# Maxima and exponentials ahead of the rounding of folded weights in steps 0 to 2 of an attention and expert layer

## The chip, the cores and the metric

One core of a Trainium2 chip runs the whole layer in one launch. The metric is the device time of an execution in microseconds (us), lower is better. The kernel before took 949.34 us, the median of 3 runs (948.89 to 950.56).

## The reference

The layer is one pre-norm block on x of 8 x 512 x 128, all in fp32. First attention with 16 heads of 64, whose keys and values come through a low-rank projection; then a mixture of 8 experts of which each token uses 2.

```python
h = layernorm(x)
kv = (h @ w_kv_down) @ w_kv_up            # 128 -> 128 -> 2048
k, v = kv[..., :1024], kv[..., 1024:]
q = h @ w_q                               # 128 -> 1024
att = softmax(causal(q k^T * 64 ** -0.5)) # 16 heads of 64, 512 x 512
x = x + (att v) @ w_out                   # 1024 -> 128
h = layernorm(x)
# logits = h @ Wr; the two largest, softmax over them
x = x + sum over the 2 chosen experts e of weight_e * (silu(h @ Wg[e]) * (h @ Wu[e])) @ Wd[e] * 12 ** -0.5
```

## The kernel before, in words

The kernel writes each engine's program out by hand, one block per engine: SyncE (SP) for most loads and stores, GpSimd (POOL), ScalarE (ACT), VectorE (DVE) and TensorE (PE). Each engine works strictly through its own list, and the lists meet through counting semaphores: `seen(eng, S[...], n)` or `wait_ge` makes an engine stop until a counter has reached n.

**Folded weights.** The product of w_kv_down and w_kv_up is made once, on chip: `fold` (L918) lets PE multiply one 512-column part (k0, v0, v1, k1) into PSUM. So that matmuls can run on a faster fp32 format without loss, every operand is held as a rounded high part and a low part that is the remainder. `w_hi` (L434) is ScalarE's rounding of a 512-column half of a weight into `Wb`, and counts `whi_done`; `w_lo` (L623) is VectorE's subtraction of that from the original, also into `Wb`, and counts `wlo_done`. The second halves of k and q are `w_lo(Wk, 1, 5, ...)`, from PSUM bank `post_ps`, and `w_lo(Wq, 1, 6, ...)`, from `w_q_sb`, which lies in SBUF in the space of `W_ffn`. The q and k of a step are split in the same way by `qk_hi` (ScalarE, L454) and `qk_lo` (VectorE, L657).

**Steps.** Attention runs in 64 steps: 8 batch rows with 8 pairs of heads each. A step n works on one pair for 512 tokens, in four pieces i of 128 queries, whose keys grow with i from 128 to 512, in the order 1, 0, 2, 3. For each piece: scores on PE (L970), maxima on VectorE with the causal mask added (`maxes`, L639), exponentials on ScalarE (`exps`, L465), reciprocal of their sums on VectorE (`inv`, L646), normalisation on GpSimd (`norm`, L333), transposes on PE (L984), their copy to SBUF on VectorE (`t_copy`, L651; piece 3 on ScalarE, `t3_copy`, L471). In the step after, PE multiplies by V (`values`, L997), ScalarE copies the result (`y_copy`) and PE projects it (`project_out`, L1004). One step ahead PE projects q and k (`project`, L925 to L927), three ahead V (`v_chunk`, the same lines), copied by ScalarE (L476).

**The opening.** Step 0 is written out apart from the others on each engine: ScalarE's from `qk_hi(0)` (L527) on, VectorE's from `qk_lo(0)` (L796) on, PE's from `fold("k0", ...)` on (L1081). PE's list there is: scores of step 0, fold v0, q and k for step 1, fold v1, four V chunks, transposes of pieces 1, 2 and 0, fold k1, transposes of piece 3, then the common `step`. The transposes of piece 2 wait for VectorE's copy of piece 1's. The matmuls of step 1's scores wait for nothing of the second halves of k and q; `project(4)`, which PE issues in step 3, waits for `wlo_done` 6.

**Other queues.** SyncE waits for `wlo_done` 6 as well (L249) and then loads the experts' first weights, 16 loads, into `W_ffn` (L251, L252); then it waits for all nine fills before it loads the second ones (L255). GpSimd issues a fill of the routed rows in DRAM (`fill`, L367) behind the normalisations of each of the steps 0 to 7, and a last one, and waits for all nine (L391) before step 9. From step 54 on the expert weights are split into high and low parts in the same way (`split_hi` L510, `split_lo` L707). After attention a table of the routed rows is made and 71 tiles of 128 rows go through the experts.

Of the kernel before, what the change touches and what calls it, by code (L numbers as in the profile page):

```python
# [16 lines left out]
B, T, C = 8, 512, 128  # L17
# [27 lines left out]
def seen(eng, sem, count):  # L45

    if not isinstance(count, int) or count > 0:
        eng.wait_ge(sem, count)
# [11 lines left out]
def layer(nc, x, w_down, w_up, w_q, w_out, Wr, Wg, Wu, Wd, out):  # L60
    ctx = ExitStack()
    with ctx:
# [88 lines left out]
        w_q_sb = W_ffn[:, 2, :]  # L151
        w_down_sb = W_ffn[:, 4, 0:R]

        Wq, Wk, Wv = ([Wb[:, a, :] for a in blocks] for blocks in ((2, 3), (6, 7), (0, 4)))
# [6 lines left out]
        post_ps = ctx.enter_context(nc.psum_tensor("post_ps", [P, T], F32))  # L161
# [22 lines left out]
        def p_at(i, h):  # L184

            o = 128 * i * (i + 1) + h * 128 * (i + 1)
            return prob[:, o:o + 128 * (i + 1)]
# [242 lines left out]
        def _(act):  # L430
# [3 lines left out]
            def w_hi(W, half, ps=None):  # L434

                if ps is None:
                    act.wait_ge(w_in[f"q{half}"], 16)
                    ps = w_q_sb[:, half * T:(half + 1) * T]
                nc.scalar.activation(W[0][:, half * T:(half + 1) * T], ps, ACT.Copy).then_inc(S["whi_done"], 1)
# [10 lines left out]
            def qk_hi(n):  # L450

                for a in range(2):
                    seen(act, S["qk_ready"], 2 * n + a + 1)
                    nc.scalar.activation(qk_sb[:, 0, a, :], mid_ps[:, a * T:(a + 1) * T], ACT.Copy).then_inc(S["qkhi_done"], 1)  # L454
# [6 lines left out]
            def exps(n, i):  # L461

                for h in range(2):
                    seen(act, S["max_done"], 8 * n + 2 * POS[i] + h + 1)
                    nc.scalar.activation(p_at(i, h), p_at(i, h), ACT.Exp, bias=neg_max[:, i, h:h + 1], scale=-1.0,  # L465
                                         accum_out=row_sum[:, i, h:h + 1]).then_inc(S["exp_done"], 1)
# [6 lines left out]
            def v_copy(n, half, t, bank=0):  # L473

                seen(act, S["v_ready"], n + 1)
                nc.scalar.activation(v_sb[:, half, t, :], mid_ps[:, bank * T:(bank + 1) * T], ACT.Copy).then_inc(S["v_copied"], 1)  # L476
# [51 lines left out]
            step0 = [(t % 2, t) for t in range(NT)]  # L528
            exps(0, 1)
            exps(0, 0)  # L530
            act.wait_ge(S["kv_ready"], 2)
            w_hi(Wv, 0, post_ps[:, :])
            exps(0, 2)
            qk_hi(1)
            act.wait_ge(S["kv_ready"], 3)
            w_hi(Wv, 1, post_ps[:, :])
            for bank, t in step0:
                v_copy(t, 0, t, bank)
            exps(0, 3)
            act.wait_ge(S["kv_ready"], 4)  # L540
            w_hi(Wk, 1, post_ps[:, :])
            t3_copy(0)
# [54 lines left out]
        def _(dve):  # L597
            dve.wait_ge(consts, 5)

            def pre_stats(b):  # L600
                dve.wait_ge(x_in[b], 16)
                for t in range(NT):
                    nc.vector.bn_stats(stats_a[:, t, :], X[:, NT * b + t, :])\
                        .then_inc(S["stats_a"], 1)
                seen(dve, S["stats_a"], NT * b + NT)
                for t in range(NT):
                    nc.vector.bn_aggr(mv_a[:, t, :], stats_a[:, t, :]).then_inc(S["aggr_a"], 1)
# [15 lines left out]
            def w_lo(W, half, count, ps):  # L623

                dve.wait_ge(S["whi_done"], count)
                o = slice(half * T, (half + 1) * T)
                nc.vector.tensor_tensor(W[1][:, o], ps, W[0][:, o].bitcast(F32), ALU.subtract).then_inc(S["wlo_done"], 1)
# [15 lines left out]
            def inv(n, i):  # L643

                seen(dve, S["exp_done"], 8 * n + 2 * POS[i] + 2)
                nc.vector.reciprocal(row_inv[:, i, :], row_sum[:, i, :]).then_inc(S["inv_done"], 1)  # L646

            def t_copy(n, i):

                seen(dve, S[f"t{i}_ready"], n + 1)  # L650
                nc.vector.tensor_copy(pt_sb(i), pt_ps(i)).then_inc(S[f"t{i}_copied"], 1)  # L651

            def qk_lo(n):

                for a in range(2):
                    seen(dve, S["qkhi_done"], 2 * n + a + 1)
                    nc.vector.tensor_tensor(qk_sb[:, 1, a, :], mid_ps[:, a * T:(a + 1) * T], qk_sb[:, 0, a, :].bitcast(F32),  # L657
                                            ALU.subtract).then_inc(S["qklo_done"], 1)

            def step(n, k, cur=True, nxt=True, pre=None, post=None):  # L660
                if cur:
                    maxes(n, 1)
                    maxes(n, 0)
                    maxes(n, 2)
                    inv(n, 1)
                    maxes(n, 3)
                    inv(n, 0)
                    inv(n, 2)

                if n - 1 in SPLIT_AT and cur:  # L670
                    split_lo(SPLIT_AT[n - 1])
                if pre is not None and k == 1:
                    pre_stats(pre)
                if post is not None and k == 2:
                    post_x2(post)
                if pre is not None and k == 3:
                    pre_norm(pre)
                if post is not None and k == 4:
                    post_xn2(post)
                if post is not None and k == 5:  # L680
                    post_choose(post)
                if post is not None and k == 7:
                    post_weights(post)
                if cur:
                    inv(n, 3)
                    t_copy(n, 1)
                if nxt:
                    qk_lo(n + 1)
                if cur:
                    t_copy(n, 2)  # L690
                    t_copy(n, 0)

                if post is not None and k == 2:
                    post_stats(post)
                if post is not None and k == 3:
                    post_aggr(post)
                if pre is not None and k == 3:
                    pre_lo(pre)
                if post is not None and k == 5:
                    post_chosen(post)  # L700
                if post is not None and k == 6:
                    post_rows(post)

            def split_lo(e):

                dve.wait_ge(S["split_hi"], SPLIT_ORDER.index(e) + 1)
                nc.vector.tensor_tensor(up_lo[:, e, :], W_ffn[:, e, :], up_hi[:, e, :].bitcast(F32), ALU.subtract)\  # L707
                    .then_inc(S["split_lo"], 1)
# [88 lines left out]
            for i in (1, 0, 2):  # L797
                maxes(0, i)
            inv(0, 1)
            w_lo(Wv, 0, 3, post_ps[:, :])  # L800
            maxes(0, 3)
            inv(0, 0)
            inv(0, 2)
            qk_lo(1)
            w_lo(Wv, 1, 4, post_ps[:, :])
            inv(0, 3)
            for i in (1, 2, 0):
                t_copy(0, i)
            w_lo(Wk, 1, 5, post_ps[:, :])
            w_lo(Wq, 1, 6, w_q_sb[:, T:2 * T])  # L810
            for k in range(1, NP + 1):
                step(k, k, pre=1)
            for m in range(1, B - 1):
# [398 lines left out]
```

## Time and profile before

| | |
|---|---|
| median of 3 runs | 949.34 us (948.89 to 950.56) |
| profiled execution, its own time | 950.33 us |
| its span, first to last instruction | 948.5 us |
| PE busy | 882.4 us, 93% |
| VectorE busy | 665.7 us, 70% |
| ScalarE busy | 620.1 us, 65% |
| GpSimd busy | 541.9 us, 57% |
| chain of work that ended last | PE 79%, VectorE 13%, GpSimd 4% |

The profile is of one execution. Its span is a little shorter than the execution's time, which has some 1.8 us around it. PE is the weight-streaming matrix engine; a busy PE is a PE with matmuls in flight. A timeline row gives start and length in us, the engine, the line of the kernel, the operation, what it writes and reads, how many instructions were merged, and in brackets the idle time of the engine before it and what ended it. "PEclk" or the granted clock is the share of full speed that TensorE's clock had.

### The profile page before, as it was taken

What the parts mean: (1) busy time and instruction counts of PE and PEld (TensorE: products, weight loads), DVE (VectorE), ACT (ScalarE), POOL (GpSimd) and SP (SyncE); (2) the same over time, 40 slices, a digit from 0 to 9 for tenths busy, and PEclk for the clock granted to TensorE, in tenths of its full rate; (3) what the DMA queues carried; (4) which work ended last, traced back from release to release, by engine and by line L of the source; (5) the groups of instructions that cost most, each with busy time, mean ns of one, the idle gap of its engine ahead of it and who ended that gap; (6) DMA issues with size and microseconds to landing.
All of it is one profiled execution on the core that took longest, in us unless ns stands there. A gap on an engine that the chain in (4) does not pass through costs nothing.

```text
span 948.5 us, 20447 instructions
## 1 busy us (share of the span) xinstructions
PE 882.4 (93%) x6126; PEld 647.6 (68%) x6127; DVE 665.7 (70%) x2442; ACT 620.1 (65%) x1614; POOL 541.9 (57%) x536
## 2 busy tenths in 40 slices
PE   6799999999999999999999999999842999999996
PEld 3566666676666667676666767676522888888885
DVE  3576788878788887878888787877853444554552
ACT  3577687777768777776877777777721455445553
POOL 3455544585566558556655855665553466665555
PEclk9999999999999999999999999999975999999998
DMA  6585430000000000000000000000011233333332
GB/s 180 181 326 212 184 101 1 1 24 13 1 11 26 1 2 23 12 2 12 24 1 1 25 12 1 11 26 1 2 34 37 35 48 49 45 45 45 45 44 28
DMA packets 43996, 44.36 MB, mean 47 GB/s; under 512 B 4352, under 2 KB 35968, under 8 KB 43920
## 3 DMA queue, kind: packets, MB, share of 16 engines
q0 software_dynamic: 16528, 26.03, 11.4%
q1 hardware_dynamic: 27392, 17.39, 6.7%
q8 instruction: 40, 0.66, 0.3%
q14 instruction: 36, 0.29, 0.1%
HBM read 15.28 MB, written 28.12 MB: 46 GB/s over the span
## 4 chain that ended last, share of the span: by engine, by line
PE 79%; DVE 13%; POOL 4%; issue 2%; ACT 1%; DMA 0%; POOLq 0%; SPq 0%; DVEq 0%
PE low_ps L997 11%; PE low_ps L984 7%; PE low_ps L1149 7%; PE mid_ps L925 7%; DVE prob L639 6%; PE top_ps L984 6%; PE mid_ps L927 6%; PE mid_ps L926 6%; PE out_ps L1004 5%; PE mid_ps L970 4%; PE out_ps L1141 4%; PE low_ps L970 4%; PE top_ps L970 3%; DVE routed L733 2%; DVE PT L613 2%
## 5 line engine op out<-in xcount | busy, mean ns | idle before, releaser
L333 POOL TENSOR_TENSOR prob<-prob,row_inv 128x512 f32<-128x512 f32 (+3 forms) x256 | 321.6, 1273 | 263.2 <-DVE row_inv L646 263.2
L465 ACT ACTIVATE prob<-prob,neg_max 128x256 f32<-128x256 f32 (+3 forms) x512 | 280.6, 550 | 10.3 <-DVE neg_max L639 3.8
L997 PE MATMUL low_ps<-PT,v_sb 128*64 128x512 f32 (+3 forms) x1024 | 152.0, 439 | 2.1 <-ACT PT L471 1.2
L997 PEld LDWEIGHTS low_ps<-PT,v_sb 128*64 128x64 f32 x1024 | 68.1, 136 | 94.1 <-issue 60.4
L414 POOL DMA_INDIRECT out<-prob,meta_row x71 | 110.6, 1558 | 36.2 <-issue 35.7
L651 DVE COPY PT<-low_ps 128x512 f32<-128x512 f32 (+1 forms) x128 | 104.6, 817 | 31.9 <-PE low_ps L984 30.8
L984 PEld LDWEIGHTS low_ps<-ident,prob 128*128 128x128 f32 x640 | 75.2, 141 | 57.7 <-POOL prob L333 27.5
L882 DVE TENSOR_TENSOR prob<-mid_ps,prob 128x512 f32<-128x512 f32 x71 | 49.1, 692 | 91.6 <-ACT prob L570 84.6
L476 ACT ACTIVATE v_sb<-mid_ps 128x512 f32<-128x512 f32 x64 | 38.3, 598 | 103.0 <-PE mid_ps L927 102.8
L639 DVE CUSTOM_DVE_ANT_0 prob<-mid_ps,mask 128x128 f32<-128x128 f32 (+1 forms) x256 | 93.7, 421 | 6.7 <-PE mid_ps L970 0.8
L984 PE MATMUL low_ps<-ident,prob 128*128 128x128 f32 x640 | 92.2, 275 | 6.2 <-DVE PT L651 5.2
L465 ACT ACTIVATION_READ_ACCUMULATOR prob<-prob,neg_max 128x1 f32 x512 | 95.6, 187 | 0.0
L471 ACT ACTIVATE PT<-top_ps 128x1024 f32<-128x1024 f32 x64 | 65.7, 1027 | 44.6 <-PE top_ps L984 44.6
L639 DVE CUSTOM_DVE_ANT_0 prob<-low_ps,mask 128x256 f32<-128x256 f32 x128 | 49.2, 422 | 54.6 <-PE low_ps L970 54.6
L657 DVE TENSOR_TENSOR qk_sb<-mid_ps,qk_sb 128x512 fp32r<-128x512 f32 x128 | 81.9, 679 | 2.9 <-ACT qk_sb L454 2.9
L564 ACT ACTIVATE xT_sb<-post_ps 128x128 fp32r<-128x128 f32 x71 | 19.8, 278 | 95.1 <-PE post_ps L1120 95.1
L639 DVE CUSTOM_DVE_ANT_0 prob<-top_ps,mask 128x512 f32<-128x512 f32 x128 | 81.9, 678 | 0.0
L349 POOL DMA_INDIRECT routed_rows<-routed,row_i x64 | 64.0, 1001 | 16.5 <-issue 16.5
L454 ACT ACTIVATE qk_sb<-mid_ps 128x512 fp32r<-128x512 f32 x128 | 67.9, 580 | 3.2 <-PE mid_ps L927 3.2
L1004 PE MATMUL out_ps<-y_sb,Wo_sb 128*128 128x512 f32 x128 | 66.7, 603 | 2.1 <-ACT y_sb L459 2.1
L984 PE MATMUL top_ps<-ident,prob 128*128 128x128 f32 x512 | 67.1, 274 | 0.7 <-POOL prob L333 0.7
L970 PE MATMUL mid_ps<-qk_sb 64*128 64x128 f32 (+1 forms) x768 | 66.2, 305 | 0.0
(172 smaller groups left out, 1773.7 us busy)
## 6 DMA issues: line engine op xcount, KB each, us to landing
routed_rows<-W_dn POOLq DMA_DIRECT2D x8, 2080.0 KB, 8.9
routed<-routed_rows SPq DMA_DIRECT2D x71, 65.0 KB, 1.9
X<-in_L_attn_x SPq DMA_DIRECT2D x8, 256.0 KB, 5.5
W_ffn<-in_L_ffn_Wg SPq DMA_DIRECT2D x8, 256.0 KB, 5.1
W_ffn<-in_L_ffn_Wu SPq DMA_DIRECT2D x8, 256.0 KB, 5.4
W_dn<-in_L_ffn_Wd SPq DMA_DIRECT2D x8, 256.0 KB, 4.6
out<-X SPq DMA_DIRECT2D x8, 256.0 KB, 2.3
out<-prob,meta_row POOLq DMA_INDIRECT x71, 3.3
```

The costliest lines, as they stand in the source:

```text
L333: nc.gpsimd.tensor_tensor(p_pair(i), p_pair(i), row_inv[:, i, :].unsqueeze(2).to_broadcast([P, 2, P * (i + 1)]), ALU.mult).then_inc(S["nor ...
L414: nc.gpsimd.indirect_dma_start(out=out, out_offset=bass.IndirectOffsetOnAxis(ap=meta_row[:, q:q + 1], axis=0), in_=eo_sb[q], in_offset=Non ...
L454: nc.scalar.activation(qk_sb[:, 0, a, :], mid_ps[:, a * T:(a + 1) * T], ACT.Copy).then_inc(S["qkhi_done"], 1)
L465: nc.scalar.activation(p_at(i, h), p_at(i, h), ACT.Exp, bias=neg_max[:, i, h:h + 1], scale=-1.0, accum_out=row_sum[:, i, h:h + 1]).then_in ...
L639: nc.vector.tensor_tensor_reduce(out=p_at(i, h), in0=scores_at(i, h), in1=mask[:, T - w:T], scale=-SCALE, scalar=BIG, op0=ALU.add, op1=ALU ...
L651: nc.vector.tensor_copy(pt_sb(i), pt_ps(i)).then_inc(S[f"t{i}_copied"], 1)
L657: nc.vector.tensor_tensor(qk_sb[:, 1, a, :], mid_ps[:, a * T:(a + 1) * T], qk_sb[:, 0, a, :].bitcast(F32), ALU.subtract).then_inc(S["qklo_ ...
L925: nc.tensor.matmul(dst, ws[0], vs[0], start=start, stop=False, **kw)
L970: last = nc.tensor.matmul(scores_at(i, h), qk_sb[d, a, 0, i * P:(i + 1) * P], qk_sb[d, b, 1, 0:P * (i + 1)], start=(k == 0), stop=(k == 2))
L984: last = nc.tensor.transpose(pt_ps(i)[:, h, j, :], p_at(i, h)[:, j * P:(j + 1) * P], ident[:, :])
L997: last = nc.tensor.matmul(y_ps[h * HD:(h + 1) * HD, j * P:T], v_sb[:, half, j, o + h * HD:o + (h + 1) * HD], PT[:, h, j, j:NT, :].rearrang ...
L1004: nc.tensor.matmul(out_ps[:, :], Wo_sb[:, pair, :], y_sb[:, :], start=(pair == 0), stop=(pair == NP - 1), skip_group_check=True).then_inc( ...
```

## The change

On ScalarE the exponentials of piece 2 of step 0 go ahead of the rounding of the first V half, and those of piece 3 ahead of the rounding of step 1's q and k, that is ahead of the second V half's rounding and of four V copies. On VectorE the maxima of piece 3 and the reciprocals of pieces 0, 2 and 3 go ahead of the subtraction for the first V half or directly behind it, ahead of `qk_lo(1)`. The subtraction for the second k half goes from the end of step 0 to behind the copies of step 1, and that for the second q half to step 2, behind the maxima and ahead of the reciprocal of piece 3. PE's, GpSimd's and SyncE's programs are the same.

```diff
--- before.py
+++ after.py
@@ -528,15 +528,15 @@
             step0 = [(t % 2, t) for t in range(NT)]
             exps(0, 1)
             exps(0, 0)
+            exps(0, 2)
             act.wait_ge(S["kv_ready"], 2)
             w_hi(Wv, 0, post_ps[:, :])
-            exps(0, 2)
+            exps(0, 3)
             qk_hi(1)
             act.wait_ge(S["kv_ready"], 3)
             w_hi(Wv, 1, post_ps[:, :])
             for bank, t in step0:
                 v_copy(t, 0, t, bank)
-            exps(0, 3)
             act.wait_ge(S["kv_ready"], 4)
             w_hi(Wk, 1, post_ps[:, :])
             t3_copy(0)
@@ -671,6 +671,8 @@
                     split_lo(SPLIT_AT[n - 1])
                 if pre is not None and k == 1:
                     pre_stats(pre)
+                if n == 2:
+                    w_lo(Wq, 1, 6, w_q_sb[:, T:2 * T])
                 if post is not None and k == 2:
                     post_x2(post)
                 if pre is not None and k == 3:
@@ -690,6 +692,8 @@
                     t_copy(n, 2)
                     t_copy(n, 0)
 
+                if n == 1:
+                    w_lo(Wk, 1, 5, post_ps[:, :])
                 if post is not None and k == 2:
                     post_stats(post)
                 if post is not None and k == 3:
@@ -797,17 +801,15 @@
             for i in (1, 0, 2):
                 maxes(0, i)
             inv(0, 1)
-            w_lo(Wv, 0, 3, post_ps[:, :])
             maxes(0, 3)
             inv(0, 0)
             inv(0, 2)
+            w_lo(Wv, 0, 3, post_ps[:, :])
+            inv(0, 3)
             qk_lo(1)
             w_lo(Wv, 1, 4, post_ps[:, :])
-            inv(0, 3)
             for i in (1, 2, 0):
                 t_copy(0, i)
-            w_lo(Wk, 1, 5, post_ps[:, :])
-            w_lo(Wq, 1, 6, w_q_sb[:, T:2 * T])
             for k in range(1, NP + 1):
                 step(k, k, pre=1)
             for m in range(1, B - 1):
```

## Rows read from the trace of the kernel before

**Rows 1.** The page: each engine's busy time, share of the span, instructions.

```profile
PE 882.4 (93%) x6126; PEld 647.6 (68%) x6127; DVE 665.7 (70%) x2442; ACT 620.1 (65%) x1614; POOL 541.9 (57%) x536
```

**Rows 2.** PE's timeline: start, length, line, operation, count, idle time before and its end.

```profile
25.58 0.50 PE L925 MATMUL mid_ps<-Wb,XT 128*128 128x512 f32 x1 [1.41 <-DVE qk_sb L657]
...
28.73 0.60 PE L984 MATMUL low_ps<-ident,prob 128*128 128x128 f32 x4
...
31.86 1.17 PE L984 MATMUL low_ps<-ident,prob 128*128 128x128 f32 x6 [2.53 <-DVE PT L651]
...
36.27 0.62 PE L970 MATMUL low_ps<-qk_sb 64*128 64x256 f32 x6
...
44.03 1.13 PE L1004 MATMUL out_ps<-y_sb,Wo_sb 128*128 128x512 f32 x2 [0.25 <-ACT y_sb L459]
...
47.53 0.62 PE L970 MATMUL low_ps<-qk_sb 64*128 64x256 f32 x6
...
56.51 1.04 PE L984 MATMUL top_ps<-ident,prob 128*128 128x128 f32 x8
```

**Rows 3.** ScalarE's timeline in steps 0 and 1.

```profile
22.16 0.61 ACT L465 ACTIVATE prob<-prob,neg_max 128x384 f32<-128x384 f32 x1
...
23.36 1.07 ACT L454 ACTIVATE qk_sb<-mid_ps 128x512 fp32r<-128x512 f32 x2
...
29.43 0.71 ACT L465 ACTIVATE prob<-prob,neg_max 128x512 f32<-128x512 f32 x1
...
37.30 0.62 ACT L439 ACTIVATE Wb<-W_ffn 128x512 fp32r<-128x512 f32 x1
...
39.02 0.51 ACT L465 ACTIVATE prob<-prob,neg_max 128x256 f32<-128x256 f32 x1 [1.10 <-DVE neg_max L639]
```

**Rows 4.** VectorE's timeline in steps 0 to 2.

```profile
24.26 1.27 DVE L657 TENSOR_TENSOR qk_sb<-mid_ps,qk_sb 128x512 fp32r<-128x512 f32 x2
...
30.96 0.17 DVE L646 RECIPROCAL row_inv<-row_sum 128x2 f32<-128x2 f32 x1 [4.84 <-ACT prob L465]
...
31.05 0.67 DVE L651 COPY PT<-low_ps 128x512 f32<-128x512 f32 x1
...
37.96 0.69 DVE L627 TENSOR_TENSOR Wb<-W_ffn,Wb 128x512 fp32r<-128x512 f32 x1 [1.43 <-ACT Wb L439]
...
48.30 0.43 DVE L639 CUSTOM_DVE_ANT_0 prob<-low_ps,mask 128x256 f32<-128x256 f32 x1 [1.11 <-PE low_ps L970]
...
53.28 0.17 DVE L646 RECIPROCAL row_inv<-row_sum 128x2 f32<-128x2 f32 x1 [1.23 <-ACT prob L465]
```

**Rows 5.** PE in half-microsecond slices: slice, length, busy, granted clock, DMA share, GB/s.

```profile
32.00:32.50 0.50, 0.50 (x5) 0.74 0.00 0
...
33.00:33.50 0.50, 0.50 (x4) 0.50 0.00 0
...
35.50:36.00 0.50, 0.50 (x6) 0.85 1.01 408
```

**Rows 6.** GpSimd's timeline, four places.

```profile
24.36 2.04 POOL L333 TENSOR_TENSOR prob<-prob,row_inv 128x256 f32<-128x256 f32 x2 [3.25 <-DVE row_inv L646]
...
52.07 3.89 POOL L333 TENSOR_TENSOR prob<-prob,row_inv 128x256 f32<-128x256 f32 x3 [0.24 <-DVE row_inv L646]
...
121.54 1.03 POOL L333 TENSOR_TENSOR prob<-prob,row_inv 128x512 f32<-128x512 f32 x1 [4.31 <-DVE row_inv L646]
...
600.49 3.00 POOL L333 TENSOR_TENSOR prob<-prob,row_inv 128x256 f32<-128x256 f32 x2 [0.24 <-DVE row_inv L646]
```

**Rows 7.** VectorE's timeline at the split of an expert weight.

```profile
600.39 1.20 DVE L707 TENSOR_TENSOR XT<-W_ffn,Wb 128x1024 fp32r<-128x1024 f32 x1
```

**Rows 8.** SyncE's timeline, its waits for wlo_done and for the fills behind it.

```profile
38.67 0.34 SPq L251 DMA_DIRECT2D W_ffn<-in_L_ffn_Wg  x1
...
118.60 5.91 SPq L255 DMA_DIRECT2D W_dn<-in_L_ffn_Wd  x8
```

**Rows 9.** Windows of 2 us, all engines: busy each, granted clock, DMA share, GB/s.

```profile
104.00:106.00 2.00, 1.98 (x11) 1.10 (x10) 1.31 (x3) 1.44 (x3) 2.00 (x2) 1.00 0.00 0
```

## The prediction

> **What bounds the kernel now.** I read the page first: PE is busy 882.4 of 948.5 us [rows 1], so a microsecond can be won only where PE stands still, where it runs slowly, or by letting its unbroken work begin sooner. Then I read PE's timeline. From about 44 us on, PE passes from step to step with hardly a gap; from one step's first scores matmul (36.27, then 47.53) to the next is a fixed round, and whatever is won before step 2 should shift all that follows. The change touches only the stretch from 19 to 54 us, so that is where I look.
>
> In it PE stands still at three places that the change could reach: 1.41 us ahead of the first V matmul at 25.58, 2.53 us ahead of the transposes of piece 2 at 31.86, and, in step 1, in the long round from the scores at 36.27 to the output projection at 44.03, 7.76 us [rows 2]. The 2.53 us gap is a chain through four engines. ScalarE first takes the exponentials of piece 3 at 29.43, since it has them behind four V copies; VectorE stands 4.84 us waiting for them, for its reciprocal at 30.96, and the copy of piece 1's transposes, ready since 29.33 (28.73 + 0.60), is queued behind it and starts at 31.05; PE's next transposes want that copy [rows 2, 3, 4].
>
> The clock is the second thing to see. PE's granted clock is full until the gap, goes to the lower level at about 32.26 (0.74 over the slice 32.0 to 32.5 is 52% at full and 48% at half) and is back at about 35.65 (0.85 over 35.5 to 36.0); between them the slices read 0.50, 1.2 GHz in place of 2.4 [rows 5]. PE was busy all through those 3.4 us, so at full clock the same work takes half, 1.7 us less. The 1.41 us gap before 25.58 brought no such fall.
>
> **The change part by part.**
>
> *Exponentials of pieces 2 and 3 earlier on ScalarE, V rounding behind them.* Piece 2's go into time in which ScalarE waited for PE's fold of the first V half; that rounding still ends where the row at 22.16 starts. Piece 3's then take about 1.4 us of ScalarE (two of 0.71 from 29.43; VectorE is released at 30.96) and the q and k roundings of step 1 start at 22.16 + 1.41 = 23.57 in place of 23.36, 0.2 us later [rows 3, 4]. VectorE starts the subtraction on them at 23.57 + 0.60 = 24.17; before, it started at 24.26, because the maxima of piece 3 lay behind the V subtraction [rows 3, 4]. Now those maxima come first, in time that VectorE spent waiting for ScalarE's V rounding, and the V subtraction still follows that rounding at once. So the V matmuls start within 0.1 us of 25.58. I cost this at nothing. Its bounds: 0.1 us won, and 0.3 us lost if the reciprocal of piece 3, which now stands ahead of the q and k subtraction, is released late.
>
> *The reciprocal of piece 3* is made at about 23.8, and what waited behind it at 30.96 is free. The copy of piece 1's transposes starts when PE has made them, 29.35; PE starts 0.81 us after a copy starts (31.05 to 31.86), so at 30.16 [rows 2, 4]. Won: 31.86 - 30.16 = **1.7 us**. GpSimd's normalisations for pieces 0, 2 and 3 must be there: the first two took 2.04 us from 24.36 and can now only be earlier, and the third takes 3.89 - 2.04 = 1.85 (all three of a step are 3.89), so even with the old start all is done by 28.3 [rows 6]. GpSimd's first fill DMA then goes out some 5 to 7 us sooner, which can only bring the end of the fills forward.
>
> *The clock.* The idle time before these transposes is now 0.83 us, less than the 1.41 us that caused no fall. So I take the clock to stay full, and the slow stretch goes: **1.7 us**. Bounds: 0, if it falls all the same, and 1.7, since all of it is gone then.
>
> *The k and q subtractions out of the end of step 0.* At 37.96 VectorE made the last of them (q), released only by ScalarE's rounding at 37.30, and the maxima of step 1 stood behind it, though their scores were ready at 36.9; ScalarE's first exponential of step 1 was at 39.02, 2.75 us behind the scores' start at 36.27 [rows 2, 3, 4]. Now the maxima start with the scores, and ScalarE is late next: the q rounding is still ahead of its exponentials, starts 1.03 us behind the scores' start (37.30) and takes 0.53 of its time (half of the pair of 1.07 at 23.36), so the first exponential comes at +1.56. From the first exponential to the projection it is 44.03 - 39.02 = 5.01 us of ScalarE's own work, unchanged: 6.57 in place of 7.76. Won: **1.2 us**. Bounds: 0.4 (if something else holds the maxima for two thirds of that) and 1.4 (PE's own round).
>
> *The k subtraction in step 1* costs VectorE 0.6 us behind its last copy; there VectorE was idle for 1.11 us until the maxima at 48.30 [rows 4]. Hidden, 0.5 us to spare; with that cover gone it would cost 0.6. *The q subtraction in step 2* stands ahead of a reciprocal for which VectorE waited 1.23 us, at 53.28 [rows 4]. Hidden, 0.6 to spare. Nothing uses the second halves of q and k before the projection for step 4, which PE issues in step 3.
>
> It does meet GpSimd, though. A subtraction with both inputs in SBUF at 600.39 (1.20 us) ran beside two normalisations of the same widths together that took 3.00 us, where such two take 2.04 at 24.36: GpSimd lost 0.96 us, and VectorE nothing [rows 6, 7]. The q subtraction is such an instruction of half the length, and starts with the normalisations of step 2 (52.07, 3.89 us, ending 55.96), so these end about 0.5 us later, at 56.45; PE wants the last of them at 56.51 [rows 2, 6]. Cost 0, bound 0.5. The Trainium skill has this as a rule (SBUF — State Buffer, section "SBUF: two separate sides"): VectorE with two SBUF inputs and a GpSimd instruction that reads SBUF exclude one another for the whole instruction, whichever comes first. The trace agrees for the case with VectorE first; if GpSimd came first with two normalisations, VectorE would by that rule wait 2.04 us, 1.4 more than it has to spare, and the sum would be 3.2 us.
>
> *The expert weights.* SyncE waits for the sixth subtraction before it loads them: from 38.67 to about 48, some 9 us later [rows 8]. They are first used in step 54. Cost nothing.
>
> **Sum:** 1.7 + 1.7 + 1.2 = 4.6 us. The profiled execution took 950.33 us (span 948.5 and 1.8 around it), so a like one would take 945.7. The median of the runs shown is 949.34, 1.0 lower; I take the difference from that: **944.7 us**.
>
> **The rivals.**
>
> *The clock is not saved* (12%). Either it falls after 0.83 us too, or it does not fall in every execution of the kernel before: the runs shown spread over 1.7 us, as much as one slow stretch costs, and the profiled one, which holds a fall, is the second slowest of the four. If so, most executions win only the waits. Then 2.9 us are won, 946.4. The Trainium skill says that the gate's moments are not tied to the kernel, so that one kernel shows different numbers of slow matmuls (TensorE: Matmul & The Clock Gate, "What's actually happening"); no two executions are shown here by which to test it.
>
> *The gain is given back* (8%). PE stands still again between attention and the experts, with the clock low, and the execution could regain its clock there a slow stretch later, 1.7 us; together with only the 2.9 us above it is 948.1, no measurable change. Or a wait that I do not see takes the place of the reciprocal's: the row of 4.84 us hides what else was late behind it. Against it: the other inputs of those transposes are ready 4 us before.
>
> *Slower, by the fills* (4%). GpSimd stops before step 9 until all nine fills of the routed rows have landed. They had by 118.60, when SyncE's next loads went out on the same condition, and were needed at 121.54, 2.9 us of margin [rows 6, 8]. The expert weights, 16 loads of 256 KB, now fall on the fills some 9 us later. If that made the last fill late by more than 2.9 us, each further microsecond would hold the normalisations and PE. To be slower than before it must be more than 2.9 + 4.6 us late; 10 us late gives 951.8. Against it: between two fills the queues are empty (share 0.00 from 104 to 106 us), so the backlog is gone long before [rows 9].
>
> *The change doesn't do what it says* (4%): the order on one engine moves and another, later wait decides; within 1 us of before, 948.5.
>
> **How the numbers follow.** Forecast 72%. A measurement of this kernel can tell about 0.2%, 1.9 us, from no change. The forecast and the first rival lie beyond it with room (4.6 and 2.9 us), with some loss for the spread of the runs: faster 0.86; the second and the last give within 0.2%: 0.10; slower 0.04. The range reaches down to 943.2, the sum with its bounds of gain (0.3 us) and the spread of the median (some 1 us), and up to 947.3, the first rival with the same spread.
>
> **What would show it.** Right: the idle time ahead of the transposes of piece 2 is 0.8 us and no slice around 30 to 36 us has a clock under 1.00; the first V matmul stays at 25.5; the scores of step 1 start at 32.9, the first exponential of step 1 1.6 us later, the first projection at 39.4 and the scores of step 2 at 42.9; in step 2 GpSimd's three normalisations take 4.4 in place of 3.89 us; the expert weights go out at 48. Wrong: a fall of the clock in front of the V matmuls; VectorE late for the maxima of step 2; a gap on PE in step 2 ahead of the transposes of piece 3; GpSimd waiting for a DMA before step 9; or a low clock that lasts longer in the stage before the experts.

## The result and the profile after

| | before | after |
|---|---|---|
| median, measured together, 20 runs each | 951.0 us (948.89 to 953.77) | 947.99 us (945.48 to 950.70) |
| ratio after to before, 95% interval | | 0.9971 (0.9961 to 0.9981) |
| profiled execution, its own time | 950.33 us | 946.45 us |
| its span | 948.5 us | 944.7 us |
| PE busy | 882.4 us | 880.3 us |

The change is faster by 0.29%, 3.0 us (1.8 to 3.7 by the interval), where 4.6 was forecast. In the range's own terms the time missed it, 947.99 against at most 947.3; of that, 1.7 us is the kernel before, whose median over 20 runs is 951.0 and not the 949.34 of the first three.

The part of the page of the kernel after that answers to [rows 1], each engine's busy time:

```profile
PE 880.3 (93%) x6126; PEld 646.6 (68%) x6127; DVE 666.2 (71%) x2442; ACT 620.4 (66%) x1614; POOL 542.4 (57%) x536
```

PE's timeline of the kernel after in steps 0 to 2, the lines that answer to [rows 2] (start, length, line, operation, count, idle time before and its end):

```profile
15.74 0.62 PE L972 MATMUL low_ps<-qk_sb 64*128 64x256 f32 x6 [1.41 <-DVE qk_sb L657]
...
21.20 1.13 PE L923 MATMUL post_ps<-W_ffn,wdT 128*128 128x512 f32 x2 [0.77 <-DVE Wb L627]
...
23.69 0.50 PE L927 MATMUL mid_ps<-Wb,XT 128*128 128x512 f32 x1 [1.36 <-DVE qk_sb L657]
...
26.84 0.60 PE L986 MATMUL low_ps<-ident,prob 128*128 128x128 f32 x4
...
28.32 0.84 PE L986 MATMUL low_ps<-ident,prob 128*128 128x128 f32 x6 [0.87 <-DVE PT L651]
...
31.04 0.63 PE L972 MATMUL low_ps<-qk_sb 64*128 64x256 f32 x6
...
37.58 1.12 PE L1006 MATMUL out_ps<-y_sb,Wo_sb 128*128 128x512 f32 x2
...
41.08 0.63 PE L972 MATMUL low_ps<-qk_sb 64*128 64x256 f32 x6
...
50.07 1.04 PE L986 MATMUL top_ps<-ident,prob 128*128 128x128 f32 x8
```

What to see: the wait ahead of the transposes of piece 2 is 0.87 us in place of 2.53. From the scores of step 1 to the projection there are 37.58 - 31.04 = 6.54 us (before 7.76), and PE does not wait for the projection any more. From the scores of step 1 to those of step 2 it is 10.04 us, before 11.26. But the first V matmul starts at 23.69, not at 25.5, and there is a new wait of 0.77 us ahead of the v1 fold. This execution differs from that of [rows 2] before the change comes into play: its first six score matmuls of step 0 took 0.62 us at 15.74, and in the profile before they took 1.01:

```profile
15.73 1.01 PE L970 MATMUL low_ps<-qk_sb 64*128 64x256 f32 x6 [1.41 <-DVE qk_sb L657]
```

ScalarE's timeline of the kernel after, answering to [rows 3]:

```profile
19.85 0.58 ACT L439 ACTIVATE Wb<-post_ps 128x512 fp32r<-128x512 f32 x1
...
20.32 0.71 ACT L465 ACTIVATE prob<-prob,neg_max 128x512 f32<-128x512 f32 x1
...
21.73 1.06 ACT L454 ACTIVATE qk_sb<-mid_ps 128x512 fp32r<-128x512 f32 x2
...
32.07 0.62 ACT L439 ACTIVATE Wb<-W_ffn 128x512 fp32r<-128x512 f32 x1
...
32.59 0.50 ACT L465 ACTIVATE prob<-prob,neg_max 128x256 f32<-128x256 f32 x1
```

Piece 3's exponentials (20.32, two with 0.71 between their starts) stand between the V rounding and the roundings of q and k at 21.73. In step 1 the first exponential starts at 31.04 + 1.55, behind the q rounding, as forecast (1.56).

VectorE's, answering to [rows 4]:

```profile
21.86 0.17 DVE L646 RECIPROCAL row_inv<-row_sum 128x2 f32<-128x2 f32 x1 [0.72 <-ACT prob L465]
...
22.34 1.29 DVE L657 TENSOR_TENSOR qk_sb<-mid_ps,qk_sb 128x512 fp32r<-128x512 f32 x2 [0.31 <-ACT qk_sb L454]
...
27.48 0.69 DVE L651 COPY PT<-low_ps 128x512 f32<-128x512 f32 x1 [3.25 <-PE low_ps L986]
...
40.66 0.68 DVE L627 TENSOR_TENSOR Wb<-post_ps,Wb 128x512 fp32r<-128x512 f32 x1
...
41.86 0.42 DVE L639 CUSTOM_DVE_ANT_0 prob<-low_ps,mask 128x256 f32<-128x256 f32 x1 [0.52 <-PE low_ps L972]
...
45.52 0.67 DVE L627 TENSOR_TENSOR Wb<-W_ffn,Wb 128x512 fp32r<-128x512 f32 x1
...
46.83 0.17 DVE L646 RECIPROCAL row_inv<-row_sum 128x2 f32<-128x2 f32 x1 [0.64 <-ACT prob L465]
```

The copy at 27.48 waits for PE alone. Both moved subtractions (40.66 and 45.52) are hidden, with 0.52 and 0.64 us of idle time left behind them.

GpSimd's in step 2 and SyncE's, answering to [rows 6, 8]:

```profile
45.63 4.33 POOL L333 TENSOR_TENSOR prob<-prob,row_inv 128x256 f32<-128x256 f32 x3 [0.24 <-DVE row_inv L646]
...
46.23 0.34 SPq L251 DMA_DIRECT2D W_ffn<-in_L_ffn_Wg  x1
...
112.32 5.49 SPq L255 DMA_DIRECT2D W_dn<-in_L_ffn_Wd  x8
```

The three normalisations of step 2 take 4.33 us in place of 3.89, by the subtraction at 45.52, and nothing waits for them: the transposes of piece 3 at 50.07 have no idle time before them.

At the scores of step 2 this trace is 47.53 - 41.08 = 6.45 us ahead of the one before, at the end of the span only 3.8. The start of each step's scores, which I read from both timelines, shows where 2.1 us went: steps 17, 25, 41 and 56 took 10.90, 10.77, 10.83 and 10.75 us in place of 10.23, 10.21, 10.24 and 10.48. So neither the 6.45 nor the 3.8 is the price of the change. The experiments had to take chance and change apart.

### The profile page after: what moved, and what is told of

It reads as the page before. It is cut to its first block, busy times and chain, and to the rows that moved or that the text cites. A ratio compares the mean times of both kernels' runs of the same rounds, so it can differ in the third digit from the quotient of the medians.

```text
span 944.7 us, 20447 instructions
## 1 busy us (share of the span) xinstructions
PE 880.3 (93%) x6126; PEld 646.6 (68%) x6127; DVE 666.2 (71%) x2442; ACT 620.4 (66%) x1614; POOL 542.4 (57%) x536
## 4 chain that ended last, share of the span: by engine, by line
PE 77%; DVE 12%; issue 4%; ACT 3%; POOL 2%; POOLq 0%; DMA 0%; SPq 0%; DVEq 0%
PE low_ps L999 10%; PE low_ps L986 7%; PE low_ps L1151 7%; PE mid_ps L927 6%; DVE prob L639 6%; PE top_ps L986 6%; PE out_ps L1006 6%; PE mid_ps L929 5%; PE mid_ps L928 5%; PE out_ps L1143 4%; PE mid_ps L972 4%; PE low_ps L972 4%; PE top_ps L972 3%; DVE PT L613 2%; ACT prob L465 2%
## 5 line engine op out<-in xcount | busy, mean ns | idle before, releaser
L651 DVE COPY PT<-low_ps 128x512 f32<-128x512 f32 (+1 forms) x128 | 104.6, 817 | 34.9 <-PE low_ps L986 34.1
```

## The experiments

Each kernel was measured beside the kernel before on the same chip. Three chips were used, and the medians of the kernel before were 947.98, 947.87 and 947.62 us there. Where a range in us is given for a difference, it is worked out from the 95% interval of the ratio. In all traces I read the same six places in the opening; "slow" is a PE whose six matmuls of step 0's first scores take 1.01 us, "fast" one where they take 0.62.

| trace | PE in step 0 | first V matmul | wait ahead of piece 2's transposes | clock behind it | scores of step 1 | of step 2 |
|---|---|---|---|---|---|---|
| before | slow | 25.58 | 2.53 | falls | 36.27 | 47.53 |
| before, second | fast | 22.92 | 2.53 | stays | 31.94 | 43.20 |
| before, third | fast | 22.91 | 2.53 | stays | 31.95 | 43.20 |
| after | fast | 23.69 | 0.87 | stays | 31.04 | 41.08 |
| after, second | fast | 23.70 | 0.88 | stays | 31.05 | 41.10 |
| after, third | fast | 23.66 | 0.88 | stays | 31.01 | 41.05 |
| order alone | slow | 25.26 | 0.88 | stays | 32.62 | 43.88 |
| subtractions alone | slow | 24.79 | 2.53 | stays | 33.80 | 43.85 |
| busy gap | slow | 25.24 | 0.69 | stays | 34.27 | 45.53 |
| copy first | slow | 24.70 | 0.88 | stays | 33.32 | 44.58 |
| q and k first | fast | 22.37 | 0.88 | stays | 29.73 | 39.77 |
| before with fillers | fast | 21.13 | 2.53 | falls | 31.82 | 43.07 |
| after with fillers | fast | 21.88 | 0.87 | stays | 29.24 | 39.28 |
| q and k first, with fillers | fast | 20.58 | 0.88 | stays | 27.93 | 37.98 |

"Stays" and "falls" speak of the stretch behind that wait alone; later falls are told further down. One column less another takes the chance of the opening out: from the first V matmul to the scores of step 1 it is 9.0 us in every kernel with the old order and no fall, 10.7 where the clock fell, and 7.35 with the new order. So the wait is worth 1.65 us and a fall 1.7.

### The order of step 0 alone

The changed kernel, with the two subtractions back where they were:

```diff
             for i in (1, 2, 0):
                 t_copy(0, i)
+            w_lo(Wk, 1, 5, post_ps[:, :])
+            w_lo(Wq, 1, 6, w_q_sb[:, T:2 * T])
...
-                if n == 2:
-                    w_lo(Wq, 1, 6, w_q_sb[:, T:2 * T])
...
-                if n == 1:
-                    w_lo(Wk, 1, 5, post_ps[:, :])
```

> Only the new order inside step 0 (exponentials, maxima and reciprocals ahead of the V rounding); the k and q subtractions stay at the end of step 0. Theory A (my sum: the wait is 1.7 us, and a fall of the clock in the gap costs another 1.7): the gap ahead of the transposes of piece 2 shrinks from 2.5 to 0.8 us, no slice from 26 to 38 us has a clock under 1.00, and the execution is 3.4 us shorter than before. Rival B (the fall of the clock in that gap is not in every execution of the kernel before): the same trace, but the median is nearer to 1.7 to 2.5 us shorter. Rival C (what was won at the opening is lost again in steps in which GpSimd issues scatters): less than 1.5 us shorter, with single steps some 0.6 us longer than 10.2.

Measured: 945.61 us against 947.98, ratio 0.9979 (0.9967 to 0.9992), so 2.0 us shorter (0.8 to 3.1). PE's timeline of this kernel:

```profile
15.75 1.01 PE L970 MATMUL low_ps<-qk_sb 64*128 64x256 f32 x6 [1.41 <-DVE qk_sb L657]
...
25.26 0.50 PE L925 MATMUL mid_ps<-Wb,XT 128*128 128x512 f32 x1 [1.36 <-DVE qk_sb L657]
...
29.89 0.85 PE L984 MATMUL low_ps<-ident,prob 128*128 128x128 f32 x6 [0.88 <-DVE PT L651]
...
32.62 0.64 PE L970 MATMUL low_ps<-qk_sb 64*128 64x256 f32 x6
...
35.73 1.73 PE L997 MATMUL low_ps<-PT,v_sb 128*64 128x512 f32 x8 [0.92 <-DVE neg_max L639]
```

The wait is 0.88 us, and nothing falls behind it; the wait of 0.92 us ahead of the values in step 1 is left, since the subtractions still stand ahead of the maxima. The amount is rival B's: 1.65 us for the wait and little more. Theory A's 3.4 lies outside the interval, if by little.

### The subtractions alone

```diff
-            w_lo(Wk, 1, 5, post_ps[:, :])
-            w_lo(Wq, 1, 6, w_q_sb[:, T:2 * T])
...
+                if n == 2:
+                    w_lo(Wq, 1, 6, w_q_sb[:, T:2 * T])
...
+                if n == 1:
+                    w_lo(Wk, 1, 5, post_ps[:, :])
```

> Only the k and q subtractions moved to steps 1 and 2; the order inside step 0 is the old one. Theory A: 1.2 us shorter than before, the 2.5 us gap is still there, with a slow clock behind it in some or all executions; from the scores of step 1 to the scores of step 2 it is 10.0 in place of 11.3 us. Rival: 0, if the q rounding on ScalarE, which still stands ahead of step 1's exponentials, sets them all the same.

Measured: 947.06 us, ratio 0.999 (0.9977 to 1.0003): not to be told from 0, and in keeping with 1.2 us. Step 1 shows it: 10.05 us to the scores of step 2 in place of 11.26, so 1.21 us. What matters more is PE's timeline ahead of that, and PE in windows of 2 us (window, length, busy, granted clock, DMA share, GB/s):

```profile
31.07 0.85 PE L986 MATMUL low_ps<-ident,prob 128*128 128x128 f32 x6 [2.53 <-DVE PT L651]
```

```profile
29.00:31.00 2.00, 0.00 (x0) 1.00 0.00 0
...
31.00:33.00 2.00, 1.93 (x12) 1.00 0.00 0
...
33.00:35.00 2.00, 2.00 (x26) 1.00 0.63 258
```

The same wait of 2.53 us as in [rows 2], on a kernel whose step 0 has the old order, and the clock stays at 1.00; six transposes take 0.85 us, not 1.17. The same wait need not bring the fall.

### The gap filled

The kernel before, with matmuls in the gap:

```diff
-            for i in (1, 2, 0):
+            transposes(0, 1)
+            pe.wait_ge(S["wlo_done"], 4)
+            for _ in range(8):
+                nc.tensor.matmul(post_ps[:, :], XT[:, 0, 0:P], Wv[0][:, 0:T], start=True, stop=True)
+            for i in (2, 0):
                 transposes(0, i)
```

> The kernel before, with eight matmuls of 128 x 128 by 128 x 512, whose result nobody reads, in PE's gap behind the transposes of piece 1 in step 0 (about 1.9 of the 2.5 us). No wait is taken away, so what it wins is the clock alone. Theory A: the clock does not fall, scores of step 1 start 1.7 us sooner, 1.7 us shorter than before in the median. Rival B: no fall in this trace either, but the median less than 1 us shorter, since the fall is in only a part of the executions of the kernel before. Rival D (the fillers take time of their own): slower than before.

Measured: 947.20 us, ratio 0.999 (0.9976 to 1.0004), 0.8 us shorter by the medians. The interval reaches from 2.3 us shorter to 0.4 longer. So this run doesn't decide: theory A's 1.7 us in every execution is inside it, and rival B's less than 1 us is nearest. What speaks for rival B is the kernel with the order alone and the traces with the whole wait and no fall. With a slow PE in step 0 the first V matmul starts at 25.24; with nearly the same rise of the clock the new order has 25.26 (order alone). So with a slow PE the change's order costs the V matmuls nothing, as I had costed it.

### The changed kernel again, twice

> The changed kernel a second time. If the opening is what the sum said, the waits are as in the first trace (0.8 to 0.9 us ahead of the transposes of piece 2, 10.0 us from the scores of step 1 to those of step 2), whatever the clock does at the start. Theory E (the 2.2 us lost between steps 16 and 58 in its first trace is chance of the moment at which GpSimd's scatters meet VectorE): this time other steps are long, or none. Rival F (the change brings it, by the place at which it leaves the engines to one another): steps 17, 25 and 41 take 10.8 to 10.9 us again in place of 10.2.

> The changed kernel a third time, beside the one with q and k first. Theory: the waits give 1.65 + 1.2 = 2.9 us in every execution and the clock in the gap 1.7 us in a part of them, so that the median is 3 to 4.5 us shorter than before; the trace has the waits of the first two (0.87 and 0.88 us ahead of the transposes of piece 2, 10.0 us from the scores of step 1 to those of step 2). Rival F (steps 17, 25 and 41 long by the change) would show 10.8 us there again.

Measured: 943.55 us against 947.98, ratio 0.9958 (0.9943 to 0.9972), and 945.00 against 947.87, ratio 0.9967 (0.9954 to 0.9979). So 4.4 and 2.9 us, after 3.0 in the first measurement; the three intervals overlap from 0.9961 to 0.9972. Both traces have the opening of the first to 0.05 us (scores of step 2 at 41.10 and 41.05), and steps 17, 25 and 41 take 10.22 to 10.24 us and step 56 10.46 and 10.48, as in the kernel before: theory E, not the rival. VectorE in step 17, in the first trace of the changed kernel and then in the second:

```profile
195.82 0.42 DVE L639 CUSTOM_DVE_ANT_0 prob<-low_ps,mask 128x256 f32<-128x256 f32 x1
...
197.25 0.29 DVE L639 CUSTOM_DVE_ANT_0 prob<-mid_ps,mask 128x128 f32<-128x128 f32 x1 [1.00 <-PE top_ps L972]
```

```profile
195.85 0.42 DVE L639 CUSTOM_DVE_ANT_0 prob<-low_ps,mask 128x256 f32<-128x256 f32 x1
...
196.36 0.29 DVE L639 CUSTOM_DVE_ANT_0 prob<-mid_ps,mask 128x128 f32<-128x128 f32 x1
```

The same maximum stands 1.00 us in the one, and follows at once in the other. GpSimd's timeline of the first shows a scatter that it was issuing, and VectorE's instruction starts 0.04 us after that ends (196.25 + 0.96 = 197.21):

```profile
196.25 0.96 POOL L349 DMA_INDIRECT routed_rows<-routed,row_i  x1 [0.30 <-issue]
```

Of 14 traces only that one has it, and in the second a scatter of the same length, from 195.95 to 196.91, held nothing up. Whether the one engine held the other there, and by what, stays open.

### The kernel before again, twice

> The kernel before again, one look at its clock. Rival B: the fall behind the 2.5 us gap depends on the moment, since the kernel with the subtractions alone had the same gap (2.53) and no fall. Then some of these looks have a fall between 28 and 36 us and scores of step 1 at 36.3 - x, and others none; if each has it, theory A stands and the other kernel was an exception.

> As the look before it: fall behind the gap or none. The wait ahead of the transposes of piece 2 is 2.5 us in both cases.

Measured: 947.42 and 947.17 us, one execution each, too few for a verdict on the time; what they are for is the trace. PE and then ScalarE and VectorE of the first of the two:

```profile
15.73 0.62 PE L970 MATMUL low_ps<-qk_sb 64*128 64x256 f32 x6 [1.41 <-DVE qk_sb L657]
...
22.92 0.50 PE L925 MATMUL mid_ps<-Wb,XT 128*128 128x512 f32 x1 [1.42 <-DVE qk_sb L657]
...
29.21 0.84 PE L984 MATMUL low_ps<-ident,prob 128*128 128x128 f32 x6 [2.53 <-DVE PT L651]
...
31.94 0.62 PE L970 MATMUL low_ps<-qk_sb 64*128 64x256 f32 x6
```

```profile
19.00 0.60 ACT L439 ACTIVATE Wb<-post_ps 128x512 fp32r<-128x512 f32 x1 [0.28 <-PE post_ps L921]
...
20.69 1.07 ACT L454 ACTIVATE qk_sb<-mid_ps 128x512 fp32r<-128x512 f32 x2
```

```profile
21.60 1.27 DVE L657 TENSOR_TENSOR qk_sb<-mid_ps,qk_sb 128x512 fp32r<-128x512 f32 x2
```

The wait of 2.53 us is there in both, and in neither does the clock fall behind it. And here is what my sum had missed. With a fast PE in step 0 the kernel before rounds q and k at 20.69 and starts its V matmuls at 22.92; the changed kernel rounds them at 21.73 and starts at 23.69, 0.77 us later. The rounding of the first V half is late as well, by piece 2's exponentials: it starts at 19.85 in place of 19.00, and the wait of 0.77 us ahead of the v1 fold comes from it. So with a fast PE the change is worth 43.20 - 41.08 = 2.1 us at the scores of step 2: 1.65 + 1.21 - 0.77.

### q and k ahead of piece 3's exponentials

The changed kernel with this:

```diff
-            exps(0, 3)
             qk_hi(1)
+            exps(0, 3)
...
-            inv(0, 3)
             qk_lo(1)
+            inv(0, 3)
```

> The changed kernel, with one thing turned round: the q and k roundings of step 1 and VectorE's subtraction on them go ahead of the exponentials and the reciprocal of piece 3 in step 0. In the traces of the changed kernel the first V matmul (23.69) waits 1.36 us for that subtraction, which waits for ScalarE, which makes piece 3's exponentials first (1.41 us); they are wanted by PE only 5 us later. Theory A (ScalarE's order sets the start of the V matmuls): first V matmul 0.6 us sooner where PE is still slow in step 0, 1.3 us sooner where it is not, the same gap of 0.9 us ahead of the transposes of piece 2, 0.6 to 1.3 us shorter than the changed kernel. Rival: no gain, since the reciprocal of piece 3 is then late for the copy of piece 1's transposes.

Measured: 943.86 us against 947.87, ratio 0.9961 (0.9947 to 0.9974); the changed kernel beside it 945.00. PE's timeline:

```profile
22.37 0.50 PE L927 MATMUL mid_ps<-Wb,XT 128*128 128x512 f32 x1
...
27.00 0.85 PE L986 MATMUL low_ps<-ident,prob 128*128 128x128 f32 x6 [0.88 <-DVE PT L651]
...
29.73 0.62 PE L972 MATMUL low_ps<-qk_sb 64*128 64x256 f32 x6
```

The V matmuls follow the v1 fold with no wait, 1.3 us sooner than in the changed kernel, and the wait ahead of the transposes is 0.88 as before: all of it reaches the scores of step 1 (31.04 - 29.73). So the place of piece 3's exponentials and their reciprocal set the start of the V matmuls. By the medians it is 1.1 us shorter than the changed kernel, and the runs of the two overlap (942.46 to 945.53 and 942.15 to 947.22), so that the trace shows the gain here and the time alone doesn't. The wait ahead of the v1 fold, 0.76 us, is left: the fold ends 0.8 us later than in the kernel before with a fast PE, and it is what the V matmuls follow now. I did not test a kernel with piece 2's exponentials back behind the V rounding.

### The clock of the opening taken out of the comparison

PE's idle time of the first 16 us filled in three kernels: the one before, the changed one, and the one with q and k first.

```diff
+            pe.wait_ge(consts, 7)
+            def busy(n):
+                for _ in range(n):
+                    nc.tensor.matmul(post_ps[:, 0:P], ones_bf[:, :], ones_bf[:, :], start=True, stop=True)
...
+            busy(14)
             fold("k0", top_ps[:, 0:T], 0)
+            busy(10)
             pre_T(0)
             pe.wait_ge(S["wlo_done"], 2)
+            busy(12)
             project(0, 0, 0)
+            busy(12)
```

> The kernel before, with 48 small matmuls (ones by ones, 128 x 128 x 128 in bf16, nobody reads the result) in PE's idle time of the first 16 us: 14 ahead of the k0 fold, 10 behind it, 12 ahead of the first projection, 12 ahead of step 0's scores. Theory G (chance in the opening is the moment at which PE's clock rises, 15 or 21 us): now it rises before step 0's scores in every execution, so from there to the scores of step 2 it is 27.5 us, as in the two early looks at the kernel before, the first projection is fast too (1.2 us less), the median is about 2 us shorter than before and the spread is smaller. Rival: the fillers hold up the fold or the projection, and nothing is won.

> The changed kernel with the same fillers. Theory H (what the change wins depends on the clock's state in step 0: with PE fast there, the V matmuls start 0.8 us later than in the kernel before, since ScalarE has piece 3's exponentials ahead of the q and k roundings): against the kernel before with fillers 1.65 - 0.8 + 1.2 = 2.1 us shorter, at the scores of step 2 and in the medians. Theory A (my sum) says 2.9 without the clock.

> The changed kernel with q and k first and the same fillers. Theory H: 1.3 us shorter than the changed kernel with fillers, 3.4 shorter than the kernel before with fillers, and the shortest of all, some 941.5 to 942.5 us where the kernel before is at 947.9.

Measured, against 947.62: 944.41 (ratio 0.9965, 0.9956 to 0.9975), 942.17 (0.9942, 0.9926 to 0.9958) and 940.84 us (0.9925, 0.9910 to 0.9941). The differences between them are 2.2 and 1.3 us, theory H's 2.1 and 1.3. They come from 12, 6 and 6 runs: with a spread of 942.70 to 948.12 for the kernel before with fillers and 940.59 to 943.43 for the changed one, the medians alone don't exclude my sum's 2.9. The kernel before won 3.2 us by the fillers, more than the 2 expected. At the scores of step 2, 43.07 and 39.28, the difference is 3.8, because in this trace of the kernel before the clock did fall behind the gap. This is also the slowest of the 12 executions, 948.12 us, and not a typical one. PE in half-microsecond slices there:

```profile
27.00:27.50 0.50, 0.09 (x1) 1.00 0.00 0
...
27.50:28.00 0.50, 0.50 (x4) 0.72 0.00 0
...
28.00:28.50 0.50, 0.50 (x5) 0.50 0.00 0
...
31.00:31.50 0.50, 0.50 (x5) 0.86 1.01 408
```

That is 1.7 us of the 3.8, the other 2.1 being 1.65 + 1.21 - 0.75. Five traces have the wait of 2.5 us with nothing in it, and the clock fell in two of them (before, before with fillers); eight have one of 0.9 us there, and it fell in none. That is in keeping with a change that prevents the fall; two in five against none in eight are too few to show it.

### VectorE's queue alone

The kernel before, with the copy ahead of the reciprocal:

```diff
-            inv(0, 3)
-            for i in (1, 2, 0):
+            t_copy(0, 1)
+            inv(0, 3)
+            for i in (2, 0):
                 t_copy(0, i)
```

> The kernel before, with nothing changed but VectorE's order at one place: the copy of piece 1's transposes goes ahead of the reciprocal of piece 3. Rival to the change's own way (the queue on VectorE alone made the wait of 2.5 us, and turning it there would do): the wait goes to 0.9 us, scores of step 1 start 1.65 us sooner. Theory (ScalarE's exponentials of piece 3 are late next, through the reciprocal and GpSimd's normalisation): a new wait of some 1.1 us ahead of the transposes of piece 3, 0.5 us won.

Measured: 946.79 us against 947.62, ratio 0.9996 (0.9984 to 1.0009): no difference that can be measured. PE's timeline:

```profile
29.34 0.84 PE L985 MATMUL low_ps<-ident,prob 128*128 128x128 f32 x6 [0.88 <-DVE PT L651]
...
32.29 1.10 PE L985 MATMUL top_ps<-ident,prob 128*128 128x128 f32 x8 [1.02 <-POOL prob L333]
```

The wait of 2.53 us is gone, and 1.02 us of it stand again ahead of the transposes of piece 3, now behind GpSimd: the exponentials are late themselves, not only in the way. From the first V matmul to the scores of step 1 it is 33.32 - 24.70 = 8.6 us, 0.4 won in place of 1.65. The change was right to move them on ScalarE too.

## Why the prediction was wrong

**The wait ahead of the transposes of piece 2: right.** 1.65 us of the 1.7 in every trace of the new order, through the step named: the copy starts when PE is ready.

**The k and q subtractions: right.** 1.21 us of the 1.2, ScalarE late next, and both subtractions hidden where they were put. GpSimd's loss, 0.44 us, was forecast and cost nothing. The expert weights went out at 46.23 with no trace of a late fill: SyncE's next loads, released by the last fill, were at 112.32 in place of 118.60, as early as everything else.

**The V matmuls' start: wrong.** "I cost this at nothing." The bounds were 0.1 us won and 0.3 us lost. The step took ScalarE's waiting time for PE's fold from one execution in which PE was slow in step 0:

```profile
21.66 0.60 ACT L439 ACTIVATE Wb<-post_ps 128x512 fp32r<-128x512 f32 x1 [2.07 <-PE post_ps L921]
```

There the cost is indeed nothing (25.24 and 25.26). With a fast PE that wait is 0.28 us, and the 1.2 us of piece 2's exponentials don't fit into it: "that rounding still ends where the row at 22.16 starts" fails. The V rounding starts 0.85 us late, the q and k roundings 1.04 (21.73 - 20.69: the 0.85 and the 0.2 that I had forecast for piece 3's exponentials), and the V matmuls 0.77. The kernel with q and k first wins that back, and 0.55 us more.

**The clock behind the gap: the right price, counted too often.** The term was 1.7 us for each execution. It is 1.7 us in those that have the fall, and three of the five traces with that gap have none. The kernel with the gap filled leaves its mean open up to 2.3 us, with 0.8 the nearest value. The argument for the new kernel was too weak as well: an idle time of 0.83 us is "less than the 1.41 us that caused no fall". The length of the wait doesn't settle it. Near the end of attention all 14 traces have a wait of 1.33 to 1.35 us ahead of six transposes (at 684.37 in the first of the changed kernel), and in 8 of them the clock falls there. That it fell in none of the eight behind 0.9 us may be luck in part. I had the fall that is not in every execution as the first rival and gave it 12%; its own figure, 2.9 us won, is the one nearest to the first measurement.

**The sum.** 1.65 + 1.21 = 2.9 us in every execution, less 0.8 in the part of them with a fast step 0, plus 1.7 in the part with a fall: between 2.1 and 4.6. With two in five for the fall and about half for the fast step 0 (6 of the 11 traces without fillers) it is 2.9 - 0.4 + 0.7 = 3.2 us, an estimate from few traces; the three measurements are 3.0, 4.4 and 2.9. My 4.6 was the upper end, because the one profiled execution of the kernel before was the one with everything to win.

The 4.4 is no support for the 4.6. The spans of the second and third trace of the changed kernel, 940.6 and 940.4 us, are 4.8 to 5.2 shorter than those of the second and third of the kernel before (945.6 and 945.4), but at the first expert tile they are only 1.6 to 2.4 ahead (720.10 and 719.66 against 722.01 and 721.67). The rest is won behind it, where the clock came back 4.4 and 5.0 us after that tile and not 9.7 and 9.9. No trace shows that the change brings this: the first of the changed kernel has 9.5. The second rival, a gain given back there, isn't seen either: the low clock before and in the first expert tiles lasts 34.1 us in the three traces of the kernel before, and 34.1, 30.7 and 30.7 in those of the changed one.

**The base.** I took the gain from 949.34, the median of three runs. Over 20 runs with those three among them it was 951.0, and later 947.6 to 948.0. With a spread of 5 us between single runs, the spread of 1 us that I allowed a median of three was too little. The ratio was missed by less, 0.9951 against 0.9971, still outside its interval.

**Two sums that don't come out.** By the terms named beside them the ends of the range are 944.7 - 0.3 - 1.0 = 943.4 and 946.4 + 1.0 = 947.4, where 943.2 and 947.3 stand; the measured time is outside either. And the forecast and the first rival have 0.84 between them, so that "faster" could not have 0.86 with a loss taken off.

## What to carry to other kernels

An order of work costed from one execution is right for that execution's speeds: ask of every term what it becomes when a neighbour that was slow is fast, above all at the opening of a kernel, where PE may be at either level of its clock. Work that is moved ahead into an engine's waiting time should stand behind whatever the critical engine wants soonest: here the q and k roundings before piece 3's exponentials, which gave 1.3 us more with a fast PE. And a fall of the clock seen in one trace is a chance to be counted, not a cost to be taken off whole.

## What the runs showed of the hardware that I had not expected

The executions of one kernel spread over 5 us, and PE's clock differs between their traces at four places: its rise in the opening, the fall behind the gap, the fall in the last attention steps that 8 of the 14 traces have (in the first of the changed kernel from 684 to 687.6, in the second none), and its return in the first expert tiles. The third costs nothing when it is that short: from the scores of the last step to the first expert tile it is 46.6 us in the first trace of the changed kernel and in the second. In the kernel before with fillers it lasts 10.2 us, and there the stretch takes 48.4. The last of the four differs most. The windows of PE in which the clock comes back, in the changed kernel's second trace, where the first expert tile starts at 720.10, and in that of the subtractions alone, where it starts at 722.52:

```profile
724.00:725.00 1.00, 0.65 (x3) 0.77 0.00 0
```

```profile
733.00:734.00 1.00, 1.00 (x8) 0.85 0.00 0
```

Low until 724.46 in the one and 733.3 in the other (0.77 and 0.85 of a microsecond's slice), it is 4.4 us after the first tile here and 10.8 there. From the first expert tile to the end of the span the one takes 220.5 us and the other 222.8, a difference of 2.3 that is as large as the change's gain with a fast PE. Over all 14 traces that stretch takes 220.4 to 223.7 us, shortest in the three in which the clock comes back within 5.1 us; one trace of each kernel cannot tell how much of the spread of its runs this makes. In the opening the granted clock is no guide: it reads 1.00 in every half-microsecond slice from 9 to 31.5 us of the profile before, also where its six score matmuls took 1.01 us against 0.62 in other executions. There the speed has to be read from the matmuls themselves.
